# Turning the second piece of x instead of the fourth on VectorE, and a rearranged beginning, in an expert-routing kernel

## What is computed

```python
W = weights[condition]                              # 16 matrices of 128 x 128
flat = einsum('bct,bcd->bdt', x, W)                 # rows (b, d) of 2048
logits = flat @ router_weight.T + router_bias       # 64 experts
scores = softmax(logits); top 8 of 64 are kept      # w_dense; w_sum is their sum
out = x + flat * w_sum + w_dense @ expert_bias      # expert_bias is 64 x 2048
```

## Time and profile before

| what | value |
|---|---|
| median of three runs | 585.45 us (584.56 to 586.2) |
| the profiled execution, its own time | 586.3 us |
| its span, first to last instruction | 584.4 us |
| PE busy, DVE busy | 95%, 82% of the span |
| POOL busy, ACT busy | 65%, 62% |
| share of the chain that ended last | PE 89%, DVE 4% |
| memory traffic | 153.86 MB, 263 GB/s |

### The profile page before, as it was taken

The page is one execution under the profiler, slowest core; times in us unless marked ns, Lnnn a source line. Parts: engine busy times, 40 slices in busy tenths (PEclk is TensorE's granted clock), DMA queues, the critical chain, the costliest instruction groups (busy, mean ns, idle before and its releaser), DMA issues.

```text
span 584.4 us, 12814 instructions
## 1 busy us (share of the span) xinstructions
PE 552.6 (95%) x3344; PEld 474.0 (81%) x3344; DVE 478.1 (82%) x1060; ACT 365.1 (62%) x773; POOL 381.3 (65%) x391
## 2 busy tenths in 40 slices
PE   5629999999999999999999999999999999999997
PEld 4528778888888888888888888888888888888865
DVE  3767898888888888888888888888888888888874
ACT  3465566766667676666767666676766667676652
POOL 0245757666776766677676667767666776766676
PEclk9959999999999999999999999999999999999999
DMA  8983778898888889888888988888898888889235
GB/s 253 305 271 122 228 250 271 285 322 255 282 257 282 265 279 318 259 264 267 279 273 278 311 270 270 257 282 266 282 307 253 280 270 272 275 282 310 120 146 214
DMA packets 63682, 153.86 MB, mean 263 GB/s; under 512 B 5362, under 2 KB 38130, under 8 KB 55538
## 3 DMA queue, kind: packets, MB, share of 16 engines
q1 hardware_dynamic: 63666, 153.67, 80.8%
HBM read 86.54 MB, written 67.11 MB: 263 GB/s over the span
## 4 chain that ended last, share of the span: by engine, by line
PE 89%; DVE 4%; SPq 3%; DMA 2%; issue 1%; ACT 1%; ACTq 0%; DVEq 0%
PE zt_ps L306 19%; PE xt_ps L293 13%; PE p_ps L354 12%; PE p_ps L359 11%; PE p_ps L356 10%; PE p_ps L355 10%; PE p_ps L360 10%; PE scores_ps L329 2%; DMA out_sb<-L_ffn_expert_bias 2%; PE scores_ps L338 1%; SPq L215 1%; PE scores_ps L320 1%; DVE out_sb L568 1%; DVE e_kept L547 1%; DVE xt_ps L511 1%
## 5 line engine op out<-in xcount | busy, mean ns | idle before, releaser
L649 POOL TENSOR_TENSOR x_lo<-x_sb,x_hi 128x512 fp32r<-128x512 f32 x256 | 327.1, 1302 | 156.4 <-ACT x_hi L420 155.7
L501 DVE TENSOR_TENSOR xt_lo<-xt_ps,xt_hi 128x512 fp32r<-128x512 f32 x256 | 173.7, 679 | 78.6 <-ACT xt_hi L412 78.5
L412 ACT CAST xt_hi<-xt_ps 128x512 fp32r<-128x512 f32 x256 | 149.7, 585 | 139.2 <-PE xt_ps L293 136.6
L568 DVE SCALAR_TENSOR_TENSOR out_sb<-p_ps,w_sum,x_sb 128x512 f32<-128x512 f32 x256 | 188.4, 736 | 11.4 <-PE p_ps L360 9.7
L420 ACT CAST x_hi<-x_sb 128x1024 fp32r<-128x1024 f32 x128 | 134.0, 1048 | 0.2 <-PE p_ps L360 0.2
L306 PE MATMUL zt_ps<-xt_hi,router_hl 128*128 128x256 f32 x512 | 129.0, 284 | 0.7 <-DVE xt_lo L501 0.7
L306 PE MATMUL zt_ps<-xt_lo,router_hl 128*128 128x256 f32 x512 | 128.7, 284 | 0.0
L354 PE MATMUL p_ps<-x_hi,w_hl 128*128 128x512 f32 x256 | 119.7, 468 | 2.6 <-issue 0.5
L293 PE MATMUL xt_ps<-ident,x_sb 128*128 128x128 f32 x768 | 116.5, 276 | 4.0 <-DMA x_sb<-x 4.0
L359 PE MATMUL p_ps<-expert_hl,kept_t_hi 128*128 128x512 f32 x256 | 104.1, 407 | 0.0
L306 PEld LDWEIGHTS zt_ps<-xt_hi,router_hl 128*128 128x128 f32 x512 | 97.7, 191 | 6.8 <-DVE xt_lo L501 1.2
(11 more groups left out here) (41 smaller groups left out, 357.4 us busy)
## 6 DMA issues: line engine op xcount, KB each, us to landing
out<-out_sb SPq DMA_DIRECT2D x128, 512.0 KB, 3.8
x_sb<-x SPq DMA_DIRECT2D x62, 1024.0 KB, 6.5
x_turn<-x SPq DMA_DIRECT2D x128, 128.0 KB, 6.1
x_sb<-x SPq DMA_DIRECT2D x4, 512.0 KB, 7.4
out_sb<-L_ffn_expert_bias SPq DMA_DIRECT2D x2, 512.0 KB, 9.2
x_sb<-L_ffn_router_weight SPq DMA_DIRECT2D x1, 512.0 KB, 5.5
bias_sb<-L_ffn_router_bias SPq DMA_DIRECT2D x1, 32.0 KB, 9.4
cond_sb<-itok_B SPq DMA_DIRECT2D x1, 0.2 KB
```

The lines of the kernel that those rows point to most:

```text
L412: act.copy(xt_hi[:, n % 2, :, r, :], xt_ps[v % 4][:, :].rearrange("p (q c) -> p q c", c=P)).then_inc(xt_hi_ready, 1)
L501: dve.tensor_tensor(xt_lo[:, n % 2, :, r, :], xt_ps[v % 4][:, :].rearrange("p (q c) -> p q c", c=P), xt_hi[:, n % 2, :, r, :].bitcast(F32) ...
L568: dve.scalar_tensor_tensor(out_sb[:, r, cols], p_ps[n % 2][:, :], w_sum[:, o % 2, r:r + 1], x_sb[:, (2 * o + r) % XRING, cols], ALU.mult, ...
L649: pool.tensor_tensor(x_lo[:, r, cols], x_sb[:, (2 * o + r) % XRING, cols], x_hi[:, r, cols].bitcast(F32), ALU.subtract).then_inc(x_lo_read ...
```

## The change

The piece that VectorE turns is now the second, `TURNED = 1`, that is slots 2 and 3; its relays stand behind the finishing of slots 0 and 1. TensorE's transposes of slots 6 and 7 come back, those of 2 and 3 go. The first two pairs (`EARLY = 2`) are turned by TensorE alone, their second piece through a strided view, and their turned loads are left out. The weights are kept whole (`w_all`); GpSimd splits the picked ones in three operations. GpSimd also makes the experts' low part, behind four picks. ScalarE's split of the experts stands one slot later (v = 5). The loads of the second pair stand ahead of condition and weights. In step 2 TensorE makes the pair's first transposes ahead of `turn_kept` of pair 0. The last entry is stored in four quarters.

```diff
-RELAID = 1
+EARLY = 2
+TURNED = 1
...
             def load_turned(m, o):
                 i = 4 * m + o
-                wait(sp, relaid_in_ps, 2 * RELAID * (i - 1))
+                wait(sp, relaid_in_ps, 2 * (i - EARLY - 1))
...
-                if h == 1:
-                    load_turned(0, 0)
...
-            sp.dma_start(cond_sb[:, :], condition).then_inc(cond_loaded, 16)
-            sp.dma_start(w_all, weights.rearrange("s c d -> c s d")).then_inc(w_loaded, 16)
             load(0, 1, 0)
             load(0, 1, 1)
-            load_turned(0, 1)
+            sp.dma_start(cond_sb[:, :], condition).then_inc(cond_loaded, 16)
+            sp.dma_start(w_all[:, :, :], weights.rearrange("s c d -> c s d")).then_inc(w_loaded, 16)
...
+            for n in range(PIECES):
+                cols = slice(n * PIECE, (n + 1) * PIECE)
+                sp.wait_ge(finished, PIECES * (B - 1) + n + 1)
+                sp.dma_start(out[B - 1, :, cols], out_sb[:, 1, cols]).then_inc(last_stored, 16)
...
-                if n >= PLAIN:
+                if n == TURNED and not early(m, o):
                     return
...
-                    if new:
+                    if new and i == 2 and v < 4:
+                        if v == 0:
+                            for ahead in range(4):
+                                transposes(m, i, ahead)
+                            turn_kept(m, 0)
+                    elif new:
                         transposes(m, i, v)
...
-                    if mid and v == 7:
+                    if mid and v == 7 and i != 1:
                         turn_kept(m, i - 1)
...
-                    if i == 0 and v == 7:
-                        act.wait_ge(w_loaded, 16)
-                        act.copy(w_all_hl[:, 0, :, :], w_all).then_inc(w_all_hi_ready, 1)
-                    if i == 1 and v == 4:
+                    if i == 1 and v == 5:
                         act.wait_ge(expert_loaded, 32)
                         act.copy(expert_hl[:, :], expert_sb).then_inc(expert_hi_ready, 1)
...
-                    if new and 2 * PLAIN <= v + 2 < SLOTS:
+                    if new and (v + 2) // 2 == TURNED and not early(m, i):
                         relay(m, i, v + 2)
...
+                wait(pool, logits_in_ps, 4 * m + o - 1)
                 wait(pool, p_ready, PIECES * (b - 7))
                 s = pool.value_load(cond_sb[0:1, bass.ds(b, 1)], min_val=0, max_val=S - 1)
-                pool.tensor_copy(w, w_all_hl[:, :, bass.ds(s, 1), :].rearrange("p h a d -> p h (a d)")
-                                 .bitcast(F32)).then_inc(w_hl_ready, 1)
...
+                for place in (full, w[:, 0, :]):
+                    pool.tensor_copy(place, w_all[:, bass.ds(s, 1), :].rearrange("p a d -> p (a d)")).then_inc(w_ready, 1)
+                pool.wait_ge(w_ready, 2 * b + 2)
+                pool.tensor_tensor(w[:, 1, :], full, w[:, 0, :].bitcast(F32),
+                                   ALU.subtract).then_inc(w_hl_ready, 1)
+
+            def expert_low():
+                pool.wait_ge(expert_hi_ready, 1)
+                pool.wait_ge(w_hl_ready, 4)
+                pool.tensor_tensor(expert_hl[E:2 * E, :], expert_sb[E:2 * E, :],
+                                   expert_hl[E:2 * E, :].bitcast(F32), ALU.subtract).then_inc(expert_ready, 1)
```

More of the change, by code:

```diff
@@ L58, in adaln_router @@
     PH = PIECES // 2
-    PLAIN = PIECES - RELAID
-    RUN = RELAID * P
+    PLAIN = PIECES - 1
+    RUN = P
     GROUPS = C // 32
@@ L80, in adaln_router @@
         expert_hl = sb("expert_hl", [P, T], F32R)
-        w_all_hl = sb("w_all_hl", [P, 2, S, D], F32R)
+        w_all = sb("w_all", [P, S, D])
         x_sb = sb("x_sb", [P, XRING, T])
@@ L128, in adaln_router @@
         out_stored = [sem(f"out_stored{i}") for i in range(2)]
+        last_stored = sem("last_stored")
         router_loaded = sem("router_loaded")
@@ L199, in first, with early @@
             return not is_loop(m) and 4 * m + o == 0
+        def early(m, o):
+            return not is_loop(m) and 4 * m + o < EARLY
         def loads(m, o, r):
@@ L271, in _ @@
                 for r in range(2):
-                    store(LOOPS, o, r)
-            for s in out_stored:
-                sp.wait_ge(s, 16 * B)
+                    if (o, r) != (UNROLL - 1, 1):
+                        store(LOOPS, o, r)
+            for n in range(PIECES):
+                cols = slice(n * PIECE, (n + 1) * PIECE)
+                sp.wait_ge(finished, PIECES * (B - 1) + n + 1)
+                sp.dma_start(out[B - 1, :, cols], out_sb[:, 1, cols]).then_inc(last_stored, 16)
+            sp.wait_ge(last_stored, 16 * PIECES)
+            for r in range(2):
+                sp.wait_ge(out_stored[r], 16 * (B - 2 * r))
         @block.tensor
@@ L292, in transposes @@
                     c0 = n * PIECE + q * P
-                    last = pe.transpose(xt_ps[v % 4][:, q * P:(q + 1) * P],
-                                        x_sb[:, (2 * o + r) % XRING, c0:c0 + P], ident[:, :])
+                    block_of_x = x_sb[:, (2 * o + r) % XRING, c0:c0 + P]
+                    if n == TURNED:
+                        block_of_x = x_sb[:, (2 * o + r) % XRING, n * PIECE:(n + 1) * PIECE].rearrange(
+                            "c (k j) -> c j k", k=P)[:, q, :]
+                    last = pe.transpose(xt_ps[v % 4][:, q * P:(q + 1) * P], block_of_x, ident[:, :])
                 last.then_inc(xt_in_ps, 1)
@@ L325, in score @@
                 i = 4 * m + o
-                pe.wait_ge(w_ready, 2 * i + 2)
+                pe.wait_ge(w_ready, 4 * i + 4)
                 pe.wait_ge(z_ready, i + 1)
@@ L367, in _ @@
                 q = t % (TB // 2)
-                if t < PLAIN * BLOCKS:
+                if t // BLOCKS == TURNED:
+                    block_of_router = router_sb[:, TURNED * PIECE:(TURNED + 1) * PIECE].rearrange(
+                        "e (k j) -> e j k", k=P)[:, t % BLOCKS, :]
+                else:
                     block_of_router = router_sb[:, t * P:(t + 1) * P]
-                else:
-                    j = t - PLAIN * BLOCKS
-                    block_of_router = router_sb[:, PLAIN * PIECE:T].rearrange("e (k j) -> e j k", k=P)[:, j, :]
                 last = pe.transpose(p_ps[t // (TB // 2)][:, q * E:(q + 1) * E], block_of_router, ident[0:E, 0:E])
@@ L406, in xt_high @@
                 i = 4 * m + o
-                if n < PLAIN:
-                    act.wait_ge(xt_in_ps, 2 * PLAIN * i + v + 1)
+                if early(m, o):
+                    act.wait_ge(xt_in_ps, SLOTS * i + v + 1)
+                elif n == TURNED:
+                    act.wait_ge(relaid_in_ps, 2 * (i - EARLY) + v - 2 * TURNED + 1)
                 else:
-                    act.wait_ge(relaid_in_ps, 2 * RELAID * i + v - 2 * PLAIN + 1)
+                    act.wait_ge(xt_in_ps, 2 * EARLY + 2 * PLAIN * i + (v if n < TURNED else v - 2) + 1)
                 wait(act, routed, PIECES * i + n - 1)
@@ L504, in relay @@
             def relay(m, o, v):
-                r, k = v % 2, v // 2 - PLAIN
+                r = v % 2
                 i = 4 * m + o
-                if v == 2 * PLAIN:
-                    dve.wait_ge(x_turn_loaded[o % 2], 16 * GROUPS * (2 * m + o // 2 + 1))
+                if v == 2 * TURNED:
+                    dve.wait_ge(x_turn_loaded[o % 2], 16 * GROUPS * (2 * m + o // 2))
                 wait(dve, xt_lo_ready, SLOTS * i + v - 3)
                 dve.transpose(xt_ps[v % 4][:, :].rearrange("p (q g c) -> p q g c", g=GROUPS, c=32),
-                              x_turn[:, o % 2, r, :, :].rearrange("p g (c q) -> p q g c", c=32)[
-                                  :, k * BLOCKS:(k + 1) * BLOCKS, :, :]
+                              x_turn[:, o % 2, r, :, :].rearrange("p g (c q) -> p q g c", c=32)
                               ).then_inc(relaid_in_ps, 1)
@@ L582, in step @@
                 for v in range(SLOTS):
[L584 to L592, removed]
                     if new:
@@ L626, in _ @@
             pool.wait_ge(cond_loaded, 16)
-            pool.wait_ge(w_all_ready, 1)
+            pool.wait_ge(w_loaded, 16)
             def pick_weights(m, o, r):
@@ L632, in pick_weights @@
                 w = w_hl[:, (2 * o + r) % 8, :, :]
+                full = w_sb[:, (2 * o + r) % 4, :]
+                wait(pool, logits_in_ps, 4 * m + o - 1)
                 wait(pool, p_ready, PIECES * (b - 7))
                 s = pool.value_load(cond_sb[0:1, bass.ds(b, 1)], min_val=0, max_val=S - 1)
-                pool.tensor_copy(w, w_all_hl[:, :, bass.ds(s, 1), :].rearrange("p h a d -> p h (a d)")
-                                 .bitcast(F32)).then_inc(w_hl_ready, 1)
[L637 to L640, removed]
+                for place in (full, w[:, 0, :]):
[8 more added lines that the diff above has]
+                                   expert_hl[E:2 * E, :].bitcast(F32), ALU.subtract).then_inc(expert_ready, 1)
+                pool.wait_ge(expert_ready, 1)
             def x_low(m, o, r):
@@ L658, in step @@
```

(2 more changed lines are left out.)

6 lines of the change are left out of this document (1 added, 5 removed).

## The result

| | before | after |
|---|---|---|
| median of seven runs each, in turn on one chip | 586.11 us (584.56 to 586.34) | 588.38 us (587.1 to 588.91) |
| the profiled execution, its own time; span | 586.3; 584.4 | 588.91; 587.2 |
| share of the chain that ended last | PE 89%, DVE 4% | PE 72%, DVE 14% |

The ratio is 1.0040, with an interval from 1.0027 to 1.0054: the changed kernel is slower by 2.3 us, and the forecast was 588.0 us. The profiled execution after is the slowest of its seven, 0.5 us above the median.

A forecast was written before the change was run, and what follows sets the result against it. TensorE, busy nearly throughout, was taken to bound the kernel. Steps +8.9, beginning -5.5 and end -0.9 sum to +2.5 us on 585.45, so 588.0 us; its terms reach from about 581.5 to 594.5.

The forecast's parts named there:

- its own work of 16.58 us a step: TensorE in a steady step: 17.06 us less 0.48 us lost at the first projection leaves 16.58 us of work.
- Both old waits gone, -0.48: First projection of a step: waits for a projection bank and the kept scores' low half both end, -0.48 us a step.
- +0.10 for projections that follow no projection: TensorE's steady step: one projection no longer behind another lasts 1.24 us instead of 1.14, making the step 16.68.
- The race for the score: Score in each step: VectorE's z_sum path takes 3.32 us, TensorE's 2.64, so TensorE stands 0.68 us.
- GpSimd's picks and the turned loads at nothing: Steady steps: three GpSimd operations a pick instead of two, and SyncE's turned loads needed earlier, cost nothing.
- The experts' low half holds keep: Beginning: GpSimd's operation of at most 5.2 us holds VectorE's keep of pair 0 to 34.3; norm near 35.3, -3.8 us.
- The beginning, -5.5: Start of the kernel: norm of pair 0 earlier by 3.8 us and 1.7 more after it, -5.5 us (-2 to -9).
- The shorter low clock: Beginning, after norm: a shorter wait may shorten TensorE's low clock; with VectorE's room, -1.7 us (0 to -4).
- The end, -0.9: End of the kernel: no stall at step 32's first projection and a smaller last store, -0.9 us (-0.3 to -1.5).
- the first: Rival at the score: z_sum is in time, so only the gain is left, 568.8 us; chance 0.1.
- keep is held in every step: Rival in the steps: GpSimd's x_lo locks VectorE's keep, the first projection waits again, 601.5 us; chance 0.08.
- The third: Rival at the beginning: keep isn't held and the clock stays high, -9.5 instead of -5.5, 584.0 us; chance 0.17.

The follow-up runs named there:

- the quarters: Changed kernel with GpSimd's low half of the experts made in four operations of 512 columns instead of one of 2048: 587.09 us, ratio 1.0011.
- the slots alone: Kernel before, with VectorE turning the second piece in slots 0 and 1 instead of the fourth in slots 4 and 5: 592.35 us, ratio 1.0108.
- the beginning alone: Changed kernel with the fourth piece turned again, behind finish of slots 4 and 5; new beginning, stores and picks kept: 577.29 us, ratio 0.9851.
- the first two edits: Changed kernel with z_sum moved ahead of the relay: 563.43 us, ratio 0.9602; or, separately, with relay 3 moved behind z_sum: 564.54 us, ratio 0.9624.

## Why the prediction was right, point by point

- **What bounds the kernel, and its own work of 16.58 us a step: right.** Two kernels without either wait have a step of 16.58; the next point says that its parts changed a little.
- **Both old waits gone, -0.48: right.** They went with the relays out of slots 4 and 5, and come back with them (0.45).
- **+0.10 for projections that follow no projection: there, but set off.** The projection that took 1.14 takes 1.24 in after (400.77 to 402.01). The small transposes that now stand ahead of a projection take 0.14 to it (391.51 to 391.65) and not the 0.22 of the earlier trace rows, which led to other transposes: 0.08 back, which the prediction did not see. That makes 16.60 of the 16.68, against 16.58 measured.
- **The race for the score: right in kind and order, a little short.** VectorE 3.31 us against a forecast of 3.32; TensorE 2.56 against 2.64, by the same 0.08 of the small transposes. So the wait is 0.75, not 0.68, and 0.07 goes to the restart. The step is 17.41 where the prediction had +0.33 and 17.39: +0.35. Over 27 steps, +9.4 against +8.9.
- **GpSimd's picks and the turned loads at nothing: right.** Neither shows among TensorE's waits in the steps.
- **The experts' low half holds keep: right.** Keep took 3.57 us and was let go at the end of an instruction of 4.53, where the forecast bounded that one by 5.2. The rule of the Trainium skill, SBUF — State Buffer, section Who interferes with whom, that a VectorE instruction with two SBUF inputs and a GpSimd instruction that reads SBUF keep each other out for a whole instruction, is borne out by both rows, the long one and the quarters, with GpSimd as the one that holds; no row here shows VectorE holding GpSimd. The split of the experts came at 28.61, inside the forecast's 27.4 to 29.3, and the low half ended at 35.10 instead of 34.3; but no x_lo came in between, and the norm was at 35.58, forecast 35.3. The megabyte less ahead of the experts is 4.0 us at 263 GB/s, not 3.5; neither decided, since the row of the split shows no wait for them.
- **The beginning, -5.5: right as a sum, wrong in its parts.** The prediction had 3.8 for the norm (3.5 measured) and 1.7 for the rest, with VectorE's room at keep named in it, but took beginning and slots as separable. They are not: up to pair 3 the slots alone bring 2.4, the beginning alone 8.6, and both together 5.5. That the sum came out to a tenth is luck too: where the experts' split falls differs by more than a microsecond between profiled executions.
- **The shorter low clock: uncertain.** At 40 to 44 the granted clock is 0.68 and not 0.50, but a second low stretch, 0.50, came at 24 to 28, behind the wait for the weights; the prediction did not see it.
- **The end, -0.9: -0.94 at the last step and -0.2 behind it.** SyncE's last wait went only from 2.3 to 2.0.
- **Rivals.** z_sum late, not in time: the first fell in after and was made true by the first two edits. That keep is held in every step fell: the kept scores are waited for twice in all. The third was not met in full, since the clock still fell (0.50 at 36 to 40 with the quarters), but its main part had the wrong price: with keep let go early the changed kernel has 587.09, not 584.0, with x_lo on GpSimd next in line.

## What to carry to other kernels

When work moves to another place in an engine's queue, run both queues from one common event, up to the instruction that is waited for: here two sums of four and five rows gave a wait that was 0.07 us off. A result of a few tenths of a per cent on the wrong side can be had back by the order alone: here moving one short operation ahead of a long one that TensorE doesn't wait for yet turned +0.4% into -4%. And a small net can hide two large halves of opposite sign; try each half alone, and don't add them without trying. When a gain is read from one execution's time line, look first at whether the rows ahead of the edit have moved as well: here 1.4 of 3.6 us had.

## What the runs showed of the hardware

- A VectorE operation with two inputs in SBUF, 0.2 us long, was held for 3.57 us by one GpSimd instruction of 64 x 2048; cut into four, the same work let it in between (0.32 and 1.31).
- GpSimd's subtraction of 64 x 2048 took 4.53 us in one instruction and 4.97 in four.
- From pair 0's score to the experts' split, with the same work on TensorE and ScalarE, it took 3.74 us where TensorE's granted clock at 24 to 28 was 1.00 (2.4 GHz), and 4.14, 4.93 and 5.46 us where it was 0.58, 0.57 and 0.50 (the last is its lower level, 1.2 GHz). In these three TensorE had stood 2.56, 3.67 and 2.90 us ahead of the score; in the first 2.42 us, then some transposes, then 0.64 us. A router matmul took 0.41 us at the lower clock and 0.28 at the full one, so where the clock fell, part of the price lay behind the wait. Each is one profiled execution, and they don't tell when the clock falls.
